# Indirect DMAs of three stages that wait for the one four back

## What is computed

```python
# attention over edges (src, dest)
scores = sum(q[src] * k[dest], -1) / 4 + attention_mask       # 8 heads of 16
weights = softmax of scores over the edges of one src
out = segment_sum(v[src] * weights, dest) @ Wo.T + bo
x = layernorm(x + out)
# message passing over edges (row, col) = (src, dst)
h = silu(concat(x[row], x[col], edge_features) @ eW1 + eb1)
agg = segment_sum(silu(h @ eW2 + eb2), row)
x = layernorm(x + silu(concat(x, agg) @ nW1 + nb1) @ nW2 + nb2)
```

## Time and profile before

| what | value |
|---|---|
| median of 3 runs | 6323.74 us (6316.65 to 6324.87) |
| the profiled execution, its own time | 6342.63 us |
| its span, first to last instruction | 6340.9 us |
| PE busy | 4009.8 us, 63% |
| DVE busy | 2375.7 us, 37% |
| ACT busy | 1209.7 us, 19% |
| POOL busy | 3666.3 us, 58% |

### The profile page before, as it was taken

One profiled execution on the slowest core, in us unless ns is written; L12 is line 12 of the kernel. 1 busy time (PEld: TensorE's weight loads), 2 busy tenths in 40 slices (PEclk: granted clock), 3 DMA queues, 4 the chain that ended last, 5 costly groups with the idle time before them and its releaser, 6 DMA issues. The chain is left out here.

```text
span 6340.9 us, 92597 instructions
## 1 busy us (share of the span) xinstructions
PE 4009.8 (63%) x25409; PEld 3210.9 (51%) x25410; DVE 2375.7 (37%) x6465; ACT 1209.7 (19%) x2122; POOL 3666.3 (58%) x3321
## 2 busy tenths in 40 slices
PE   6899999993333334322666556666346777777776
PEld 4555565562222222212555555555226677667764
DVE  6344434442222222257333333333253433433334
ACT  0222222220111111101111111111122333333332
POOL 0456655555666666632888888888305555555551
PEclk9975555555656556656777777777567888888888
DMA  2100000002111111111444444443411111111111
GB/s 109 58 10 10 10 10 10 10 10 68 43 42 43 43 43 41 43 26 12 36 36 35 36 36 35 36 36 35 109 50 39 37 38 38 37 37 37 36 37 51
DMA packets 278674, 238.37 MB, mean 38 GB/s; under 512 B 57254, under 2 KB 246758, under 8 KB 278245
## 3 DMA queue, kind: packets, MB, share of 16 engines
q0 software_dynamic: 198144, 170.19, 17.3%
q1 hardware_dynamic: 77604, 54.50, 2.8%
q10 hardware_dynamic: 2880, 13.11, 0.5%
HBM read 143.89 MB, written 93.71 MB: 37 GB/s over the span
## 5 line engine op out<-in xcount | busy, mean ns | idle before, releaser
L1060 POOL DMA_INDIRECT sums_dram<-we_merged_rows,we_idx x832 | 1286.1, 1546 | 427.7 <-issue 202.2
L1687 POOL DMA_INDIRECT ed_bg<-b_rows_dram,ed_idx x832 | 792.5, 952 | 676.1 <-DVE ed_idx L1695 458.2
L652 POOL DMA_INDIRECT records_dram<-rec_out,row_idx x784 | 768.6, 980 | 566.5 <-issue 284.7
L751 POOL DMA_INDIRECT sc_k<-k_rows_dram,sc_idx x832 | 802.4, 964 | 470.7 <-issue 249.9
L1212 PE MATMUL ps_merged<-we_rows,we_same_dst 128*128 128x129 f32 x1664 | 355.4, 380 | 588.4 <-issue 435.6
L1212 PEld LDWEIGHTS ps_merged<-we_rows,we_same_dst 128*128 128x128 f32 x1664 | 304.2, 273 | 623.2 <-issue 613.3
L853 PE MATMUL ps_q<-tab,sc_oht 128*128 x2496 | 361.5, 264 | 348.6 <-issue 345.0
L1832 PE MATMUL ps_ed_s<-ed_ohf,ed_efs 128*128 128x128 f32 x1664 | 433.8, 417 | 215.5 <-ACT ed_efs L1772 149.0
L853 PEld LDWEIGHTS ps_q<-tab,sc_oht 128*128 128x128 bf16 x2496 | 250.2, 104 | 458.2 <-issue 404.0
L779 DVE TENSOR_TENSOR sc_prods<-ps_q,sc_k 128x1024 f32<-128x1024 f32 x104 | 127.1, 1222 | 933.0 <-remote 911.0
L1832 PEld LDWEIGHTS ps_ed_s<-ed_ohf,ed_efs 128*128 128x128 f32 x1664 | 339.0, 232 | 258.7 <-issue 217.0
(11 more groups left out here) (288 smaller groups left out, 7889.4 us busy)
## 6 DMA issues: line engine op xcount, KB each, us to landing
sc_k<-k_rows_dram,sc_idx POOLq DMA_INDIRECT x832
sums_dram<-we_merged_rows,we_idx POOLq DMA_INDIRECT x832
ed_bg<-b_rows_dram,ed_idx POOLq DMA_INDIRECT x832
sums_dram<-zero_rows ACTq DMA_DIRECT2D x20, 640.0 KB, 8.5
records_dram<-rec_out,row_idx POOLq DMA_INDIRECT x784
co_rows<-sums_dram SPq DMA_DIRECT2D x48, 256.0 KB, 3.9
records_dram<-rfill SPq DMA_DIRECT2D x16, 416.0 KB, 6.9
records<-records_dram SPq DMA_DIRECT2D x1, 6656.0 KB, 18.8
```

What stands on the lines that cost most here:

```text
L652: pool.indirect_dma_start(c.rec_rows, bass.IndirectOffsetOnAxis(ap=idx[:, b, j:j + 1], axis=0), out[:, b, j, :], None, bounds_check=SLOTS ...
L751: pool.indirect_dma_start(kg[:, r, k * F:(k + 1) * F], None, c.k_dram[:, :], bass.IndirectOffsetOnAxis(ap=idx[:, r, k:k + 1], axis=0)).the ...
L1060: pool.indirect_dma_start(c.acc_dram[k][:, :], bass.IndirectOffsetOnAxis(ap=idx[:, r, k:k + 1], axis=0), rows[:, r, k, 0:F], None, compute ...
L1687: pool.indirect_dma_start(bg[:, r, k * F:(k + 1) * F], None, c.b_dram[:, :], bass.IndirectOffsetOnAxis(ap=idx[:, r, k:k + 1], axis=0)).the ...
```

## The change

Placing, scoring and the edge network get the pattern of weighing. There are four semaphores per stage, used in turn (`LANES = 4`). Ahead of each indirect DMA POOL waits until the semaphore that this DMA will raise shows that the DMA four back has landed, and increments a semaphore that nobody waits for, as weighing does. The consumers wait on all four semaphores instead of on the one of the buffer. Buffers, sizes, order and the number of DMAs stay.

```diff
+LANES = 4
...
-    s_sent = semaphores(nc, c.stack, "records_sent0 records_sent1")
+    s_sent = semaphores(nc, c.stack, "records_sent0 records_sent1 records_sent2 records_sent3")
+    (s_free,) = semaphores(nc, c.sems, "scatter_free")
...
-                    wait_count(dve, s_sent[b], 16 * PG * i)
+                    for n in range(LANES):
+                        wait_count(dve, s_sent[n], 16 * (PG // LANES) * (g - 1))
...
                     for j in range(PG):
+                        n = j % LANES
+                        wait_count(pool, s_sent[n], 16 * ((PG // LANES) * g + j // LANES))
+                        pool.sem_inc(s_free, 1)
                         pool.indirect_dma_start(
                             c.rec_rows, bass.IndirectOffsetOnAxis(ap=idx[:, b, j:j + 1], axis=0),
-                            out[:, b, j, :], None, bounds_check=SLOTS - 1, oob_is_err=False).then_inc(s_sent[b], 16)
+                            out[:, b, j, :], None, bounds_check=SLOTS - 1, oob_is_err=False).then_inc(s_sent[n], 16)
...
                     for k in range(SG):
+                        n = k % LANES
+                        wait_count(pool, s_k[n], 16 * (SG // LANES * g + k // LANES))
+                        pool.sem_inc(s_began, 1)
                         pool.indirect_dma_start(kg[:, r, k * F:(k + 1) * F], None, c.k_dram[:, :],
                                                 bass.IndirectOffsetOnAxis(ap=idx[:, r, k:k + 1], axis=0)
-                                                ).then_inc(s_k[r], 16)
+                                                ).then_inc(s_k[n], 16)
...
                     dve.wait_ge(s_q, g + 1)
-                    dve.wait_ge(s_k[r], ring_count(g, r, 16 * SG))
+                    for n in range(LANES):
+                        dve.wait_ge(s_k[n], 16 * (SG // LANES) * (g + 1))
...
                     for k in range(G):
+                        wait_count(pool, s_b[k], 16 * g)
+                        pool.sem_inc(s_began, 1)
                         pool.indirect_dma_start(bg[:, r, k * F:(k + 1) * F], None, c.b_dram[:, :],
                                                 bass.IndirectOffsetOnAxis(ap=idx[:, r, k:k + 1], axis=0)
-                                                ).then_inc(s_b[r], 16)
+                                                ).then_inc(s_b[k], 16)
...
                     dve.wait_ge(s_z, g + 1)
-                    dve.wait_ge(s_b[r], ring_count(g, r, 16 * G))
+                    for n in range(LANES):
+                        dve.wait_ge(s_b[n], 16 * (g + 1))
```

More of the change, by code:

```diff
@@ L651, in send @@
                     for j in range(PG):
+                        n = j % LANES
+                        wait_count(pool, s_sent[n], 16 * ((PG // LANES) * g + j // LANES))
+                        pool.sem_inc(s_free, 1)
                         pool.indirect_dma_start(
                             c.rec_rows, bass.IndirectOffsetOnAxis(ap=idx[:, b, j:j + 1], axis=0),
-                            out[:, b, j, :], None, bounds_check=SLOTS - 1, oob_is_err=False).then_inc(s_sent[b], 16)
+                            out[:, b, j, :], None, bounds_check=SLOTS - 1, oob_is_err=False).then_inc(s_sent[n], 16)
                 each_pair(pool, send)
-                for b in range(2):
-                    pool.wait_ge(s_sent[b], 16 * PG * (IT // 2))
+                for n in range(LANES):
+                    pool.wait_ge(s_sent[n], 16 * (PG // LANES) * IT)
 NG = NT // G
@@ L679, in group_at @@
     return g + by, (r + by) % RING, there
-def ring_count(g, r, each):
-    return (g - r + RING) * (each // RING)
 def load_windows(eng, c, regs, side, g, n=1):
@@ L722, in score @@
     s_k = semaphores(nc, c.stack, "sc_k_in0 sc_k_in1 sc_k_in2 sc_k_in3")
-    s_turn, s_init = semaphores(nc, c.sems, "sc_gather_turn sc_init")
+    s_turn, s_init, s_began = semaphores(nc, c.sems, "sc_gather_turn sc_init sc_gather_begun")
     SG = 2 * G
@@ L1645, in edges @@
     s_b = semaphores(nc, c.stack, "ed_b_in0 ed_b_in1 ed_b_in2 ed_b_in3")
-    (s_turn,) = semaphores(nc, c.sems, "ed_gather_turn")
+    s_turn, s_began = semaphores(nc, c.sems, "ed_gather_turn ed_gather_begun")
     K = 9 * 2 * G
```

## The result

| what | before | changed |
|---|---|---|
| median | 6323.01 us (4 runs, 6316.65 to 6324.87) | 6412.77 us (4 runs, 6395.76 to 6425.36) |
| the profiled execution, its own time | 6342.63 us | 6395.76 us |
| its span | 6340.9 us | 6394.0 us |

The ratio is 1.0142, with a 95% interval of 1.0117 to 1.0167: the change costs 90 us where 498 us of gain were forecast.

What follows compares the result with a forecast made beforehand. PE's late completions during indirect-DMA bursts were taken to stall scoring and the edge network. Gains of 206 + 272 + 20 = 498 us from the profiled 6342.6, less 18.9 to the median, gave 5826 us; range 5690 to 6350.

Steps and rivals of the forecast that it cites:

- the full cure: Scoring, edge network and placing lose their late PE completions: 498 us gained, 5826 us; chance 0.48.
- weighing's three peculiarities: Weighing's DMAs wait for the one four back with own semaphores, accumulate, and come every 1.85 us instead of 1.25.
- scoring: First to last gather falls from 1271.0 to POOL's pace, 1064.5 us: gain 206, ends 0 and 237.
- the edge network: PE bounds it at 5.7 us a group, 1186 us instead of 1458.2: gain 272, ends 148 and 401.
- The wait itself: POOL's wait for the DMA four back: landing takes at most 3.5 us, four periods 5.0, so cost 0.
- POOL's added instructions: 2448 increments, nearly all with a wait, ahead of indirect DMAs in three stages: cost 0, upper end 120 us.
- The cover: POOL's sequencer works on the added instructions while the DMA before is processed; without it some 0.05 us each.
- DVE's added waits: DVE waits for four semaphores instead of one in three stages: cost 0, at most 62 us.
- Placing: "Remote" waits are some 48 us in the stage and PE is nearly full: gain 20, between 0 and 48 us.
- The first: Rival: stalls come from gathers as such or their 1.25 us pace, so no change, 6324 us; chance 0.24.
- The second: Rival: only long runs of DMAs pushed ahead do harm; scoring gains 206, edge network nothing, 6118 us; chance 0.12.
- The third: Rival: the wait binds because landings take over 5.0 us; slower, 6407 us at 5.2 us; chance 0.16.

Runs made afterwards that it cites:

- e6: The kernel before with the change in placing alone; ratio 0.9986 against a kernel before of 5687.94 us.
- e4: The changed kernel with two semaphores instead of four, each DMA waiting for the one two back; 6491.95 us, 1.1422 against a kernel before of 5683.78 us.
- h1: The kernel before with the added POOL and DVE instructions, without holding back or made pauses; 6354.99 us, 1.0059 against a kernel before of 6315.90 us.
- e7: The kernel before with the change in scoring alone; ratio 1.0005 against a kernel before of 5687.94 us.
- g2: g1 plus the added POOL and DVE instructions, without the holding back; 6784.73 us.
- g3: The changed kernel with the same made pauses as g1; 6801.65 us.
- g1: The kernel before with POOL made to pause at every group of scoring and the edge network; 6716.61 us, kernel before 6319.60 us.
- e5: The changed kernel unaltered, run again; ratio 1.0003 against a kernel before of 5687.94 us.
- g4: g3 with the wait and increment of a group's first gather written ahead of POOL's waits for the index and DVE; 6773.38 us.

## Why the prediction was wrong

**The step that failed** is the full cure, with its 0.48: "the change gives the first" of weighing's three peculiarities "to the other three stages", taken as the one that matters. The reading of the stall held. PE's completions do reach their consumers late while indirect DMAs run, and where they don't (the prompt chips) scoring and the edge network take 638 us less. But with four DMAs in flight, each held to a landing, they are about as late as with 24 pushed ahead: "remote" is 685.1 us of the waits of DVE's product in scoring, 782.1 before, and the stage is as long, 1270.9 and 1271.0 us. What weighing has that the others lack may be one of the two things the change doesn't give, the accumulation or the pace, or something that the prediction didn't list, such as PE's own work there. None was tried.

**The sizes of the cure**, seen on prompt chips: scoring 218 us (forecast 206, from POOL's pace of 1.281 us; it ran at 1052.7 / 831 = 1.267), the edge network 420 (forecast 272), placing nothing (forecast 20). The edge network was mis-sized because I let PE bound it at 5.7 us a group, reasoning from one stretch and a lowered clock; it ran at POOL's pace, 5.0 us a group, above the upper end of 401 that I kept (831 x 1.27 from 1458.2 would have been 403). The row of its window in e6 shows where the bound went wrong:

```profile
4527.00:5566.00 1039.00, 1014.41 (x8687) 921.00 (x8686) 577.45 (x1848) 499.97 (x828) 785.64 (x832) 0.99 0.21 53
```

PE does nearly the same matmuls in 1014.4 us, 4.88 a group, at a granted clock of 0.99, where it was 5.39 at 0.85 with the stalls. The lower clock, from which I reasoned, came with the stalls and went with them. PE is then busy 98% of the stretch, so it is close to being the limit too.

**The wait itself, cost 0**: right that it doesn't slow POOL's pace, for the reason given; as part of the holding back it still comes with the 52 us, by a way that stays open. It doesn't bind at 3.4 us of the 5.0 us, and in the changed kernel on a prompt chip POOL's starts released by a landing came after 73.8 / 242 = 0.30 us. But 3.5 us was counted from start to consumer; the right sum was the landing, 2.5 us, plus some 0.9 us from there to the start. The Trainium skill ("DMA: Bandwidth & Descriptors", Anatomy of one DMA) has about 2.0 us of fixed cost and leaves that last part out. By that figure alone waiting for the DMA two back (2.5 us at this pace) would not have bound either, and the 808 us of e4 decide against that.

**POOL's added instructions, cost 0**, and **DVE's added waits, cost 0**: wrong on the late chip. The cover I named ("the sequencer works while the DMA before is processed") is gone at each pause, and I had counted pauses as POOL's waiting without asking what comes after them. There, 0.10 us on POOL in h1 (0.16 in the changed kernel) and up to 0.16 on DVE lie on the way from a landing over DVE's product or sum and the next index to the next DMA. Both bounds (120 and 62 us) held: 39 us in all. On prompt chips POOL never pauses in these two stages, and placing is as long with the longer hand-over as without (1290.7 and 1290.6 us in e6 and e7). The zeros are right there only as a sum: the edge network's 12 to 14 us are made up elsewhere.

**Placing** was forecast to gain 20 us and lost 35 in the measured pair; between g2 and g3 it is 34, by the holding back. What goes with it in the trace: PE multiplies a group's one-hots with themselves (the Gram matmuls, line 596 before), and DVE multiplies the result with a triangle of ones (line 459). Counting groups in which DVE, idle until then, starts this over 0.5 us after the recorded end of PE's last Gram matmul, between 300 and 1400 us, gives in the measured pair 12 of 83 before and 36 of 81 in the changed kernel; on the late chip 0 of 83 in g1 (whose placing is the old code), 13 of 83 in g2 and 9 of 83 in h1 with the instructions, but 37 of 81 in g3; on a prompt chip e5 has 0 of 84. A group takes 13.19 us before, 13.55 after. So with the holding back PE's Gram result more often arrives late; that this makes the longer group is my reading. Whether POOL's wait does it, or DVE's four waits on different semaphores (0.36 us, where four on one semaphore took 0.16 or 0.36), stays open.

**The rivals.** The first, that the stalls don't come from what the change alters, was right in that and had 0.24; its time was 6324 "with up to 12 more", and the extra is 90. But it put them down to the gathers or their pace, and on prompt chips the same gathers at the same pace stall nothing. The second fell with scoring's unchanged stretch. The third had the sign and, with 6407 us, nearly the number, but not the mechanism, so that its number nearly fits is luck. The gaps inside a group stayed at 0.30 us, all but seven or eight of a stage, and where a trace of the kernels above has the landings of gathers the longest took 3.9 us (e7). The trace of the changed kernel that was measured against the kernel before has none recorded.

That the stall belongs to the chip could not be seen from one trace; that it might be no property of the kernel was no case of mine. What makes PE's completions late on one chip and not on four others is open, and so is how the holding back costs its 52 us.

## What to carry to other kernels

Before you cost an added wait or increment at nothing because it is hidden behind the engine's work, look for the engine's pauses: at the end of each, every semaphore instruction between the releasing event and the next start is on the path, and one written ahead of the wait that ends the pause is not (0.88 us in g3, 0.72 in g4 and g1). Before you read an experiment as showing that a wait costs nothing, ask whether it could bind there at all: in the edge network of g3 it couldn't. When a stage with the stall and one without it differ in three ways, adopting one of them is a guess; measure which one it is first. And run the kernel before again beside each experiment: here the same kernel differed by 11% between chips, and a change that cost 1.4% where the kernel was slow cost nothing on a chip where it was fast.

## What the runs showed of the hardware

- PE's completions arrive late during bursts of indirect DMAs on one chip of five: 6316 to 6320 us against 5683 to 5691 for the same kernel. With bursts of only eight gathers that drain, the lateness of the query matmuls falls to a median of 2.8 us from 6.1 or more, but not to the 0.01 us of a prompt chip.
- From the start of a gather to the start of one that waits for its landing it takes some 3.4 us, of which the landing is 2.5 us in the median (2.4 to 3.9 us in scoring of e7); the scatters of placing land after 2.1 us, the accumulating ones of weighing after 3.3. Holding POOL to two in flight raises the pace of scoring from 1.25 to 1.68 us.
- A wait and an increment on POOL delay the indirect DMA that ends a pause by 0.10 us when the wait was met long ago, and by 0.16 us in the changed kernel; three more waits on DVE delay its next instruction by up to 0.16 us.
- The granted clock of the edge network is 0.85 with the stalls and 0.99 without them, for the same matmuls.
